# A fused two-layer transformer block on one Trainium2 core: first attention's weights as host-laid parts, fewer and larger loads, entry reordered

## What is computed

```python
# _L0_attn_ref: 16 heads of 128, no mask
w = codes * jnp.repeat(scales, 32, axis=0)        # for q, k, v (256 x 2048) and o (2048 x 256)
q = x @ wq + bq; k = x @ wk + bk; v = x @ wv + bv
scores = einsum('bqhd,bkhd->bhqk', q, k) / sqrt(128)
out = einsum('bhqk,bkhd->bqhd', softmax(scores), v) @ wo + bo
```

## Time and profile before

| | |
|---|---|
| median of 3 runs | 2058.29 us (2054.74 to 2060.03) |
| profiled execution, its time | 2058.2 us |
| its span, first to last instruction | 2056.5 us |
| granted TensorE clock, mean | 0.970 |
| TensorE matmuls busy | 1913.6 us (93%) |
| VectorE, ScalarE, GpSimd busy | 1438.9, 1178.0, 1149.5 us |
| DMA moved | 310.30 MB, 151 GB/s over the span |

### The profile page before, as it was taken

The page is one execution under the profiler, slowest core; times in us unless marked ns, Lnnn a source line. Parts: engine busy times, 40 slices in busy tenths (PEclk is TensorE's granted clock), DMA queues, the critical chain, the costliest instruction groups (busy, mean ns, idle before and its releaser), DMA issues. The chain is left out here.

```text
span 2056.5 us, 31580 instructions
## 1 busy us (share of the span) xinstructions
PE 1913.6 (93%) x10632; PEld 1497.0 (73%) x10632; DVE 1438.9 (70%) x2367; ACT 1178.0 (57%) x1939; POOL 1149.5 (56%) x856
## 2 busy tenths in 40 slices
PE   6699999999999999999999698889999898899996
PEld 5488788887887887888887577645554457788885
DVE  6587778777887877878887754477767736455555
ACT  4466666666666666666665555276666654333333
POOL 2476776776776767767765564134343445344443
PEclk9899999999999999999999999999999979899997
DMA  7877777777777777777777420000000010110001
GB/s 175 220 257 260 265 255 257 266 259 254 252 259 261 258 252 255 270 256 252 261 261 249 143 83 1 9 4 4 6 5 1 1 55 24 31 32 24 16 1 41
DMA packets 211796, 310.30 MB, mean 151 GB/s; under 512 B 16369, under 2 KB 174833, under 8 KB 211697
## 3 DMA queue, kind: packets, MB, share of 16 engines
q1 hardware_dynamic: 211696, 309.00, 45.3%
HBM read 172.64 MB, written 136.31 MB: 150 GB/s over the span
## 5 line engine op out<-in xcount | busy, mean ns | idle before, releaser
L582 POOL TENSOR_TENSOR attn_probT_lo<-attn_probT_lo,attn_probT_hi 128x1024 fp32r<-128x1024 f32 x254 | 609.2, 2399 | 256.3 <-ACT attn_probT_hi L956 256.2
L1072 DVE STREAM_TRANSPOSE attn_turned_prob<-attn_prob 128x1024 f32<-128x1024 f32 x256 | 318.1, 1243 | 193.5 <-DMA attn_spill<-attn_turned_prob 120.2
L946 ACT ACTIVATE attn_prob<-psum,attn_neg_max 128x1024 f32<-128x1024 f32 x256 | 285.7, 1116 | 243.4 <-DVE attn_neg_max L1066 242.1
L1066 DVE TENSOR_REDUCE attn_neg_max<-psum 128x1 f32<-128x1024 f32 x256 | 305.0, 1191 | 16.8 <-PE psum L81 16.7
L956 ACT ACTIVATE attn_probT_hi<-attn_probT_lo 128x1024 fp32r<-128x1024 f32 x256 | 268.8, 1051 | 1.0 <-DMA attn_probT_lo<-attn_spill 1.0
L81 PE MATMUL psum<-attn_probT_hi,attn_v_hi 128*128 128x512 f32 x512 | 211.3, 413 | 22.3 <-POOL attn_probT_lo L582 20.6
L81 PE MATMUL psum<-attn_key_hi,attn_q_hi 128*128 128x512 f32 x512 | 206.0, 402 | 26.6 <-ACT attn_prob L946 23.5
L81 PE MATMUL psum<-attn_probT_hi,attn_v_lo 128*128 128x512 f32 x512 | 206.7, 404 | 0.0
L81 PE MATMUL psum<-attn_probT_lo,attn_v_hi 128*128 128x512 f32 x512 | 205.9, 402 | 0.0
L81 PE MATMUL psum<-attn_key_hi,attn_q_lo 128*128 128x512 f32 x512 | 204.2, 399 | 0.0
L81 PE MATMUL psum<-attn_key_lo,attn_q_hi 128*128 128x512 f32 x512 | 202.0, 395 | 0.0
(11 more groups left out here) (237 smaller groups left out, 4703.5 us busy)
## 6 DMA issues: line engine op xcount, KB each, us to landing
attn_spill<-attn_turned_prob SPq DMA_DIRECT2D x256, 512.0 KB, 4.5
attn_probT_lo<-attn_spill SPq DMA_DIRECT2D x256, 512.0 KB, 5.1
attn_v_all<-in_moe_w SPq DMA_DIRECT2D x23, 384.0 KB, 3.1
acc_sb<-in_x SPq DMA_DIRECT2D x4, 512.0 KB, 6.2
x_sb<-in_wq_codes SPq DMA_DIRECT2D x8, 256.0 KB, 4.1
x_sb<-in_wq_scales SPq DMA_DIRECT2D x32, 64.0 KB, 3.6
x_sb<-in_wk_codes SPq DMA_DIRECT2D x8, 256.0 KB, 4.1
x_sb<-in_wk_scales SPq DMA_DIRECT2D x32, 64.0 KB, 4.0
```

Of the source, the lines that this page charges most:

```text
L582: engine.tensor_tensor(lo, f32(lo), f32(hi), ALU.subtract).then_inc(done, 1)
L946: nc.scalar.activation(prob[:, tile % 2, :].rearrange("p (b n) -> p b n", b=NSQ), by_key, ACT.Exp, bias=neg_max[:, tile % 2:tile % 2 + 1], ...
L1066: nc.vector.tensor_reduce(neg_max[:, tile % 2:tile % 2 + 1], scores(tile), AX.XY, ALU.max, negate=True).then_inc(max_ready, 1)
L1072: nc.vector.transpose(turned_prob[:, tile % 2, :], prob[:, tile % 2, :]).then_inc(turned, 1)
```

## The change

The host lays the weights out per pass: `w_qkvo` has, for each of 8 passes and 128 partitions, the codes of q and k, the scales of q and k (repeated 32 times, so that each partition has its own copy), then codes and scales of v, then those of wo, in 4096 columns. `b_qkv` has the three biases for each partition. A pass's loads are now five DMAs (four of 512 KB with 4 KB rows, one of 130 KB) instead of 23. They stand between two stores: after the store of tile 1, 3, 5, 9 and 21 of a pass. The `bo` rows of batch 1 are set two tiles at a time after the stores of tiles 13, 14, 17 and 18 of pass 0. In the last pass the next stage's loads come after tiles 1, 3, 6 and 17. In the entry, VectorE prepares both q and k weights before it takes the turned x, and does the statistics of groups 2 and 3 later; ScalarE normalises group 2 after it has taken q and k, and group 3 in slot 0; GpSimd scales group 3 behind the v weights; TensorE no longer waits for the biases. The statistics' room moves from `turned_prob` to the last tiles of `v_whole`.

```diff
-    LOAD_AFTER = {0: "q", 1: "k", 2: "v", 5: "o"}
+    LOAD_AFTER = {1: "qk codes", 3: "qk scales", 5: "bias", 9: "v", 21: "wo"}
+    LOAD_NEXT_STAGE = {1: "x 0", 3: "x 1", 6: "second", 17: "first"}
+    SET_ACC = {13: 0, 14: 1, 17: 2, 18: 3}
...
-        codes, scales = staged[:, 0:WQKV + WO], staged[:, WQKV + WO:]
+        qk_codes_in, qk_scales_in, v_in, wo_in = (staged[:, n * 2 * nq:(n + 1) * 2 * nq] for n in range(4))
+        codes = [qk_codes_in[:, 0:nq], qk_codes_in[:, nq:], v_in[:, 0:nq], wo_in[:, 0:nq]]
+        scales = [qk_scales_in[:, 0:nq], qk_scales_in[:, nq:], v_in[:, nq:], wo_in[:, nq:]]
...
-            def load_part(m, which, done):
-                part = bass.ds(m * HP * D0, HP * D0)
-                x = "qkv"[which]
-                to = slice(which * KC * HP * D0, (which + 1) * KC * HP * D0)
-                sp.dma_start(codes[:, to].rearrange("p (k n) -> p k n", k=KC),
-                             ins[f"w{x}_codes"].rearrange("(k p) n -> p k n", p=P)[:, :, part]).then_inc(done, 16)
-                rows = ins[f"w{x}_scales"].rearrange("(k b) n -> b k n", k=KC)
-                for b in range(P // scale_rows):
-                    sp.dma_start(scales[b * scale_rows:(b + 1) * scale_rows, to].rearrange("p (k n) -> p k n", k=KC),
-                                 rows[b:b + 1, :, part].squeeze(0).partition_broadcast(scale_rows)).then_inc(done, 16)
...
+            def weights_of(m, cols):
+                return ins["w_qkvo"][bass.ds(m, 1)].squeeze(0)[:, cols]
+            def load_weights(m, first_col, some, done):
+                cols = slice(first_col, first_col + some)
+                sp.dma_start(staged[:, cols], weights_of(m, cols)).then_inc(done, 16)
...
             def load_bias(m, done):
-                for which, x in enumerate("qk"):
-                    sp.dma_start(bias_in[:, which * HP:(which + 1) * HP],
-                                 ins[f"b{x}"][:, bass.ds(m * HP, HP)]).then_inc(done, 16)
-                sp.dma_start(bias_v_in[:], ins["bv"][bass.ds(m * HP * D0, HP * D0)].partition_broadcast(P)).then_inc(done, 16)
-            def set_acc(g):
-                sp.wait_ge(norm.turned, g + 1)
-                for t in norm.tiles(g):
-                    sp.dma_start(k.acc[:, t, :], ins["bo"].partition_broadcast(P)).then_inc(acc_set, 16)
+                sp.dma_start(bias_all[:], ins["b_qkv"][bass.ds(m, 1)].squeeze(0)).then_inc(done, 16)
+            def set_acc(t):
+                sp.dma_start(k.acc[:, t, :], ins["bo"].partition_broadcast(P)).then_inc(acc_set, 16)
...
             def next_weights(m, what):
-                if what == "q":
+                if what == "qk codes":
                     if first(m):
                         sp.wait_ge(first_w, 2)
-                        sp.wait_ge(wv_ready, 1)
                     else:
                         wait(sp, wqk_ready, m, 2, 0)
-                    load_part(m + 1, 0, landed_q)
-                    load_bias(m + 1, landed_q)
-                elif what == "k":
-                    load_part(m + 1, 1, landed_k)
+                    load_weights(m + 1, 0, 2 * nq, landed_qk)
+                elif what == "qk scales":
+                    load_weights(m + 1, 2 * nq, 2 * nq, landed_qk)
+                elif what == "bias":
+                    wait(sp, wv_ready, m, 1, 1)
+                    load_bias(m + 1, landed_qk)
                 elif what == "v":
-                    load_part(m + 1, 2, landed_v)
+                    load_weights(m + 1, 4 * nq, 2 * nq, landed_v)
                 else:
                     wait(sp, wo_ready, m, 2, 2)
-                    load_wo(m + 1, landed_o)
+                    load_weights(m + 1, 6 * nq, 2 * nq, landed_o)
+            def next_stage(what):
+                if what == "x 0":
+                    sp.wait_ge(wqk_ready, 2 * (passes - 1))
+                    after.load_x(sp, 0)
+                elif what == "x 1":
+                    after.load_x(sp, 1)
+                elif what == "second":
+                    sp.wait_ge(wv_ready, passes)
+                    mlp.load_second(sp)
+                else:
+                    sp.wait_ge(wo_ready, 2 * passes)
+                    mlp.load_first(sp)
             def store(m, tile):
                 group = m * GROUPS + tile // GT
...
+            def between(m, tile):
+                if first(m) and tile in SET_ACC:
+                    n = SET_ACC[tile]
+                    sp.wait_ge(norm.turned, QG + n // 2 + 1)
+                    for t in range(ST + 2 * n, ST + 2 * n + 2):
+                        set_acc(t)
+                if not last(m) and tile in LOAD_AFTER:
+                    next_weights(m, LOAD_AFTER[tile])
+                if last(m) and tile in LOAD_NEXT_STAGE:
+                    next_stage(LOAD_NEXT_STAGE[tile])
             def exchange(m):
                 for group in range(GROUPS):
                     tiles = range(group * GT, (group + 1) * GT)
                     for t in tiles[:3]:
                         store(m, t)
+                        between(m, t)
                     for t in tiles[:2]:
                         fetch(m, t)
                     store(m, tiles[3])
+                    between(m, tiles[3])
                     for t in tiles[2:]:
                         fetch(m, t)
-                    if first(m) and group == 1:
-                        for g in range(QG, norm.groups):
-                            set_acc(g)
-                    if not last(m) and group in LOAD_AFTER:
-                        next_weights(m, LOAD_AFTER[group])
-                    if last(m) and group == 4:
-                        sp.wait_ge(wo_ready, 2 * passes)
-                        for g in range(after.ahead):
-                            after.load_x(sp, g)
-                        mlp.load_first(sp)
-                        mlp.load_second(sp)
...
             for g in range(QG):
                 norm.load_x(sp, g)
             sp.dma_start(k.ident[:], ins["ident"]).then_inc(consts, 16)
-            load_part(0, 0, consts)
-            load_bias(0, norm.loaded[QG])
-            load_part(0, 1, norm.loaded[QG])
+            load_weights(0, 0, nq, consts)
+            load_weights(0, 2 * nq, nq, consts)
+            load_weights(0, nq, nq, landed_first)
+            load_weights(0, 3 * nq, nq, landed_first)
+            load_bias(0, landed_first)
             for g in range(QG, norm.groups):
                 norm.load_x(sp, g)
-            load_part(0, 2, landed)
-            load_wo(0, landed)
+            load_weights(0, 4 * nq, 2 * nq, landed)
+            load_weights(0, 6 * nq, 2 * nq, landed)
             for g in range(QG):
-                set_acc(g)
+                sp.wait_ge(norm.turned, g + 1)
+                for t in norm.tiles(g):
+                    set_acc(t)
             exchange(0)
             with sp.Fori(1, passes - 1) as m:
                 exchange(m)
             exchange(passes - 1)
...
-                pool.wait_ge(norm.loaded[QG], first_k)
+                pool.wait_ge(landed_first, 3 * 16)
                 nc.gpsimd.tensor_scalar(bias_qk[:, 0:HP], bias_in[:, 0:HP], scale, 1.0, ALU.mult, ALU.mult).then_inc(scale_set, 1)
                 nc.gpsimd.tensor_scalar(bias_qk[:, HP:], bias_in[:, HP:], 1.0, 1.0, ALU.mult, ALU.mult).then_inc(scale_set, 1)
                 nc.gpsimd.tensor_scalar(bias_v[:], bias_v_in[:], 1.0, 1.0, ALU.mult, ALU.mult).then_inc(scale_set, 1)
-                for g in range(QG, norm.groups):
+                norm.scale_x(pool, QG)
+                pool.wait_ge(landed, 2 * 16)
+                values = slice(2 * nq, 3 * nq)
+                nc.gpsimd.tensor_tensor(codes[2], codes[2], scales[2], ALU.mult).then_inc(split, 1)
+                pool.wait_ge(split, 1)
+                nc.gpsimd.tensor_tensor(flat(w[0])[:, values], codes[2], one[:].broadcast_to([P, nq]), ALU.mult).then_inc(split, 1)
+                pool.wait_ge(split, 2)
+                nc.gpsimd.tensor_tensor(flat(w[1])[:, values], codes[2], f32(flat(w[0])[:, values]), ALU.subtract).then_inc(wv_ready, 1)
+                for g in range(QG + 1, norm.groups):
                     norm.scale_x(pool, g)
-                values = slice(2 * nq, WQKV)
-                pool.wait_ge(landed, first_others)
-                nc.gpsimd.tensor_tensor(codes[:, values], codes[:, values], scales[:, values], ALU.mult).then_inc(split, 1)
-                pool.wait_ge(split, 1)
-                nc.gpsimd.tensor_tensor(flat(w[0])[:, values], codes[:, values], one[:].broadcast_to([P, nq]), ALU.mult).then_inc(split, 1)
...
                     after.turn(pe, g, last_turn_banks(g)).then_inc(after.turned, 1)
-            pe.wait_ge(consts, first_q)
+            pe.wait_ge(consts, 3 * 16)
...
+            act.wait_ge(scale_set, 5)
             for unit in range(4):
                 take_qk(0, unit)
-                if unit == 1:
-                    for g in range(QG, norm.groups):
-                        norm.normalise_x(act, g)
```

(27 more changed lines are left out.)

73 lines of the change are left out of this document (30 added, 43 removed).

## The result

The kernel after the change takes 2021.1 us (median of 4 runs, 2020.13 to 2025.46) against 2057.17 us (4 runs, 2054.74 to 2060.03): a ratio of 0.9828, 95% interval 0.9808 to 0.9848. That is 36 us between the medians, or 1.7% less. The profiled run took 2021.16 us, its span is 2019.4 us.

What follows compares the result with a forecast made beforehand. The prediction took TensorE to bound the stage, interrupted by blocks of loads ahead of a store. Gains of 10.5 + 14 + 5 + 6 = 35.5 us from 2058.2 gave 2022.7, said as 2023 us, range 2014 to 2037.

Steps and rivals of the forecast that it cites:

- Passes 1 to 6: Steady passes of the first attention: plain loads spread between stores remove most waits, gaining 10.5 us, bounds 3 to 11.9.
- The price of the copies: SyncE's load queue: a row copied to many partitions moves at 75 GB/s, plain rows at 300 GB/s.
- Pass 0: First pass: the 13.49 us hole and its lower clock go, less a charge; gain 14 us, bounds 7 to 17.8.
- the charge for the `bo` pairs: Pass 0: batch 1's `bo` copies, two pairs in neighbouring tiles, delay fetches beyond their slack, costing 1.2 us.
- The rival that the pairs stop pass 0 anew: Pass 0: the `bo` pairs stop TensorE again, so it gains only 7 us, 28.5 in all, 2029.5 us; chance 0.15.
- Entry: Start to first turn: the waits for biases (2.57 us) and k (3.16 us) go; gain 5 us, bounds 2 to 7.
- Last pass: Last attention pass: spreading the six loads behind tile 19 removes the 3.96 us wait and lower clock; gain 6, bounds 3 to 7.5.
- Rest: GpSimd's and ScalarE's weight work and the next stages: unchanged, 0 us.
- VectorE's waits in passes 1 to 6 stem from the order of stores and fetches: Rival for passes 1 to 6: loads are not the cause, steady gain only 1 to 3 us, total 2035 us; chance 0.12.
- plain loads run at copy speed: Rival for the new loads: a 512 KB load takes 7 us, making the kernel slower, 2074.5 us; chance 0.03.
- the holes were cover: Rival for TensorE's holes: another engine needed them, so the time stays within a few us; chance 0.03.
- The signs: Right: no TensorE wait above 3 us, store waits under 30; wrong: pass-0 stops at tiles 16 to 24, loads over 6.

## Why the prediction was right, and where its sizes were off

The forecast was 2023 us in a range of 2014 to 2037; measured 2021.1. The mechanism held: TensorE bounds the stage, the blocks of slow loads ahead of a store made the holes, and in five of the six steady passes TensorE now runs without a gap. That the total came within 2 us is partly luck: 8.8 us too little for passes 1 to 6 were made up by 2.9 too much for pass 0 and by 5.6 lost behind the stage, where nothing was changed. Term by term:

**Passes 1 to 6: 10.5 predicted, 19.3 measured.** The mis-sized step is taking the listed waits, 10.2 us, as all that loads cost TensorE there. The records of these matmuls overlap. In the timeline of before, first at full clock, then behind the wait at 509.56:

```profile
500.04 0.40 PE L81 MATMUL psum<-attn_key_hi,attn_q_hi 128*128 128x512 f32 x1
500.27 0.39 PE L81 MATMUL psum<-attn_key_lo,attn_q_hi 128*128 128x512 f32 x1
500.50 0.39 PE L81 MATMUL psum<-attn_key_hi,attn_q_lo 128*128 128x512 f32 x1
...
511.11 0.63 PE L81 MATMUL psum<-attn_key_lo,attn_q_hi 128*128 128x512 f32 x1
511.54 0.63 PE L81 MATMUL psum<-attn_key_hi,attn_q_lo 128*128 128x512 f32 x1
```

At full clock a record lasts 0.40 us, but the next one starts 0.23 us after it; at the lower clock they start 0.43 us apart. Idle time counts from the modelled end of a record, so every listed wait is 0.17 us longer than listed, and a shorter one is not listed at all. Counted from start to start, passes 1 to 6 of the kernel before lose 20.2 us in 81 gaps, 58 of them under 0.17 us; after the change they lose 0.2. Of the 20 us, 12.6 are the 15 listed waits, about 1.5 the lower clock after 509.56 (which I had counted, as 1.7; my own terms give 1.9), and some 6 are short gaps that no list shows. My upper bound of 11.9 was therefore no bound.

The price of the copies was wrong as well. I had put 1.13 MB of them at 15 us of the queue per pass, at the 75 GB/s of a window with `bo` rows. From landing to landing, scales and biases took 8.5 us per pass in the trace of before: 6.8 for 1 MB of scales, which is about 154 GB/s. The low rate held for the `bo` rows, which 128 partitions read.

**Pass 0: 14 predicted, 11.1 measured.** The hole and its clock went as said. Mis-sized is the charge for the `bo` pairs: 1.2 us, where laying the rows out gives 5.3 to 6.7. Counted from start to start, TensorE loses 4.5 us in tiles 20 to 23 after the change and nothing there with the rows laid out. The 6.7 are of an execution in which the clock did not fall after the first `weigh` either, which is worth about 1.5 us. The rate I had used was right here (66 to 76 GB/s alone); wrong was that VectorE's and TensorE's slack would take it in. Each double pair makes a store land late, and the fetches and the next store behind it: VectorE waited 1.88 and 2.19 us after the first, 3.95 and 2.61 after the second, then TensorE 2.17, and its clock was 0.57 over the next 4 us. The rival that the pairs stop pass 0 anew was thus true in its mechanism, and in size between its 7 us of gain and my 14. (With its gain of 28.5 us it should have said 2029.7, not 2029.5.) The Trainium skill, page "DMA: Bandwidth & Descriptors", section "Anatomy of one DMA — SWDGE (gpsimd) path", fits about 2 us plus bytes / 436 GB/s for a DMA that GpSimd issues; an estimate by it for 128 KB is 2.3 us. These DMAs are SyncE's and share the queue. Rows of their own come near it, with 2.9 us to landing; the one shared row, with 7.0, does not.

**Entry: 5 predicted, 5.5 measured**, but in half of it for the wrong reason. I had put 2.57 us to the biases' wait. It went in the kernel with the old orders too, and its first turn is at 34.17 us all the same: what bounded the entry was VectorE's and ScalarE's work between q and k. The size is luck in that part. The orders gave all but 0.3 us. They do need the k weights by 10.60 us: with narrow copies, the same orders reach the first turn only at 31.3 to 33.1 us.

**Last pass: 6 predicted, 6.8 measured.** 4.7 us of it are the block, as its own run showed; the other 2.1 are within the scatter of the last pass among kernels that keep the block (172.4 to 174.9).

**Rest: 0 predicted, 5.6 lost** in the profiled execution, with the same instructions. The windows of before and after, from the stage's end to the last instruction:

```profile
1186.88:2056.50 869.62, 796.52 (x5208) 579.61 (x5208) 528.53 (x1181) 438.91 (x838) 354.08 (x398) 0.95 0.06 20
```

```profile
1144.23:2019.40 875.17, 802.98 (x5208) 584.87 (x5208) 527.00 (x1181) 439.09 (x838) 353.98 (x398) 0.94 0.07 20
```

VectorE is busy 1.5 us less, ScalarE and GpSimd equally long; TensorE's 5208 matmuls take 6.5 us more at a mean granted clock of 0.94 instead of 0.95. No run shows this to be the change's doing: the kernel with `bo` in rows of 1 KB has 867.3 us there, that with narrow copies in the new places 880.1.

**Rivals.** That VectorE's waits in passes 1 to 6 stem from the order of stores and fetches and not from the loads is refuted: the layout without new places brings 17.3 of the 19.3 us there. That plain loads run at copy speed is refuted by the page's DMA issues after the change (count, KB each, us to landing), where they take little longer than a store of the same size:

```profile
attn_spill<-attn_turned_prob SPq DMA_DIRECT2D x256, 512.0 KB, 4.7
...
x_sb<-in_w_qkvo SPq DMA_DIRECT2D x30, 512.0 KB, 5.3
```

That the holes were cover is refuted by the time.

**The signs.** No wait of TensorE above 3 us, the first turn at 28.98, and no window of 2 us under 150 GB/s at full share in passes 1 to 6: right. VectorE's waits for stores under 30 us: wrong, 60.0. In passes 1 to 6 they are harmless, since TensorE has no gaps there but in the first, and they were no sign of the gain. DMA share near 1 around the `bo` pairs: wrong, 0.33 to 0.88. Two signs that I had named as against came true although the forecast held. TensorE did stop between tiles 16 and 24 of pass 0, for the 2.17 us above. And loads of 512 KB did land after more than 6 us: the one behind the store of tile 3 takes 6.3 to 6.7 us in each of passes 1 to 6, as here in pass 3 (window 451 to 452.2 us):

```profile
x_sb<-in_w_qkvo SPq DMA_DIRECT2D x1, 512.0 KB, 6.7
```

With ScalarE waiting 0.2 us in all for fetches, that was harmless.
